# Local attention with 64 keys per 32 queries, a token shift in whole rows, and the band mask written into the score banks by ScalarE

## The reference

```python
for i in range(6):
    x = attn_layer(shift_tokens(x), Wqkv[i], ...) + x      # 16 heads of 64
    x = ffn_layer(shift_tokens(x), ...) + x                # 2 x 341 wide
# shift_tokens: the upper 64 of the 128 features come from the token before
# attention: q and k are normalised per head, rotated and scaled, then
mask = (it < jb) | (it > jb + w) | (jb == -1)              # w = 32
sim = jnp.where(mask, -jnp.finfo(sim.dtype).max, sim)
attn = softmax(sim); out = einsum(attn, v)
```

## Time and profile before

| | |
|---|---|
| median of 3 runs | 1836.76 us (1835.83 to 1837.04) |
| profiled execution, its own time | 1836.35 us |
| its span in the trace | 1834.6 us |
| PE, DVE, ACT, POOL busy | 1702.5, 1604.0, 1416.7, 1533.9 us |
| share of the span | 93%, 87%, 77%, 84% |
| mean granted TensorE clock | 0.979 of full speed |

### The profile page before, as it was taken

How to read it: one execution, slowest core, us unless ns; L and a number is a source line. 1 busy time by engine, 2 the same in 40 slices (tenths; PEclk the granted TensorE clock), 3 DMA queues, 4 the chain that set the end, 5 groups by cost and what they waited for, 6 DMA issues and landing times.

```text
span 1834.6 us, 39770 instructions
## 1 busy us (share of the span) xinstructions
PE 1702.5 (93%) x14065; PEld 1372.6 (75%) x14256; DVE 1604.0 (87%) x2852; ACT 1416.7 (77%) x4889; POOL 1533.9 (84%) x2056
## 2 busy tenths in 40 slices
PE   6589999999999999999999999999999999999995
PEld 4468777787787777787777877877777777778774
DVE  4588898998998989989989999989899899899982
ACT  3278878878788787787797787887877887978872
POOL 2489988898988988988989888889888889898870
PEclk9599999999999999999999999999999999999997
DMA  3000010000010000001000001000001000000000
GB/s 114 2 1 3 3 46 2 4 17 1 8 46 1 4 17 1 8 3 44 4 1 17 8 1 46 5 1 17 4 5 46 3 2 16 1 8 4 1 4 26
DMA packets 24154, 25.38 MB, mean 14 GB/s; under 512 B 13795, under 2 KB 21654, under 8 KB 23190
## 3 DMA queue, kind: packets, MB, share of 16 engines
q1 hardware_dynamic: 23958, 22.83, 4.1%
HBM read 18.65 MB, written 1.05 MB: 11 GB/s over the span
## 4 chain that ended last, share of the span: by engine, by line
PE 71%; DVE 19%; ACT 3%; issue 3%; POOL 3%; DMA 1%; SPq 0%; POOLq 0%; DVEq 0%
PE ps L410 9%; PE ps L382 8%; PE ps L402 7%; PE ps L369 7%; PE ps L390 7%; PE ps L362 7%; PE ps L364 5%; PE ps L363 5%; DVE xh L975 4%; PE ps L377 3%; PE ps L441 3%; DVE ss L905 2%; DVE t L920 2%; DVE t L922 2%; ACT pr L620 2%
## 5 line engine op out<-in xcount | busy, mean ns | idle before, releaser
L620 ACT ACTIVATE pr<-ps,nmax 128x128 f32<-128x128 f32 x1536 | 549.2, 389 | 28.2 <-DVE nmax L939 25.4
L743 POOL TENSOR_TENSOR t<-t 128x512 f32<-128x512 f32 x384 | 500.4, 1303 | 75.7 <-DVE t L922 75.7
L777 POOL TENSOR_TENSOR pr<-pr,rsum 128x512 f32<-128x512 f32 x384 | 406.5, 1059 | 22.8 <-DVE rsum L946 22.1
L765 POOL TENSOR_TENSOR t<-t,rn 128x512 f32<-128x512 f32 x384 | 402.5, 1048 | 21.8
L620 ACT ACTIVATION_READ_ACCUMULATOR pr<-ps,nmax 128x1 f32 x1536 | 352.4, 229 | 0.0
L585 ACT ACTIVATE sq<-ps 128x512 f32<-128x512 f32 x384 | 235.4, 613 | 116.0 <-PE ps L364 112.1
L920 DVE TENSOR_TENSOR t<-ps,rope 128x512 f32<-128x512 f32 x384 | 262.3, 683 | 42.0 <-ACT sq L585 37.5
L362 PE MATMUL ps<-w_hi,xt_hi 128*128 128x512 f32 x576 | 280.1, 486 | 14.3 <-DVE t L922 10.0
L369 PE MATMUL ps<-consts,t 128*128 128x128 f32 x1536 | 239.1, 278 | 29.4 <-ACT qT L612 26.1
L922 DVE TENSOR_TENSOR t<-ps,rope 128x512 f32<-128x512 f32 x384 | 260.5, 678 | 0.0
L905 DVE TENSOR_REDUCE ss<-sq 128x8 f32<-128x512 f32 x384 | 252.0, 677 | 3.6 <-ACT sq L585 2.6
(11 more groups left out here) (121 smaller groups left out, 2879.0 us busy)
## 6 DMA issues: line engine op xcount, KB each, us to landing
wqkv<-wqkv_in SPq DMA_DIRECT2D x6, 1536.0 KB, 12.3
wo<-wo_in SPq DMA_DIRECT2D x6, 512.0 KB, 9.6
xsh<-xr SPq DMA_DIRECT2D x24, 127.0 KB
w<-w_in SPq DMA_DIRECT2D x6, 342.0 KB, 7.5
w<-w_in SPq DMA_DIRECT2D x6, 172.5 KB
x<-x_in SPq DMA_DIRECT2D x4, 256.0 KB, 4.9
out<-x SPq DMA_DIRECT2D x4, 256.0 KB, 2.9
ctx<-ctx_in SPq DMA_DIRECT2D x4, 240.0 KB, 4.5
```

Of the source, the lines that this page charges most:

```text
L620: i = A(pr[:, g, k, :], ps[:, S_BANK[odd], k * P:(k + 1) * P], ACT.Exp, bias=nmax[:, h2, odd, k:k + 1], accum_out=psums[:, h2, odd, k:k + 1])
L743: G.tensor_tensor(t1[:, c, :], t1[:, c, :], t2[:, c, :], ALU.add).then_inc(qk_added[c], 1)
L765: G.tensor_tensor(w, w, rn[:, par(u), h2, a, :].unsqueeze(2).broadcast_to([P, 8, E]), ALU.mult).then_inc(done, 1)
L777: G.tensor_tensor(w, w, rsum[:, g // 2, g % 2, :].unsqueeze(2).broadcast_to([P, 4, P]), ALU.mult).then_inc(pr_ready[g], 1)
```

## The change

Scores and probabilities are made for only 64 keys for each 32 queries: the queries 0 to 31 and 32 to 63 take the keys from 0, 64 to 95 those from 32, and 96 to 127 those from 64. The parts are these.

- `scores` runs once in a unit, for all 16 heads: each head takes four matmuls of 32 queries by 64 keys. A group of 32 queries writes PSUM partitions of its own, so a head pair takes 8 places of the array. The mask is no longer a matmul. `mask_scores` (ACT) copies it into both banks, and the matmuls add to what stands there.
- `exps` has 16 activations of 64 columns, `row_max` runs once over both banks, `normalise_p` twice.
- Two heads' probabilities of 64 columns stand side by side, so `transpose_p` has 8 transposes in a unit in place of 16 and `copy_pT` two copies in place of four.
- `weigh_values` takes 48 matmuls over 64 keys, of 64 or 32 columns, in place of 16 over 128 keys. Transposed probabilities of even heads stand on partitions 0 to 63 and those of odd heads on 64 to 127, and so must the values: `shift_v` (SP) moves rows of v into `v_win` by four transfers of 64 rows by 512 numbers (128 KB) for each unit.
- `clamp_norm`, `guess_norm` and `refine_norm` run once in a unit for all 32 sums. `copy_o` runs twice on ACT and no longer on DVE.
- `shift_tokens` moves 127 whole rows of 512 numbers, where it moved 127 x 4 pieces of 64, and `copy_half` writes the lower half again after it, so it waits for the transfer.
- The weights of Q, K and V arrive in six transfers in place of one; w1 is split in two halves; the banks are dealt anew and all four `step` lists are written in another order.

```diff
+SPAN = 64
+WINDOW_START = [0, 0, 32, 64]
+BLOCKS = H // 2
...
-    QKV_BANK = [0, 1, 1, 0, 1, 0]
-    TQ_BANK = [4, 4, 5, 5]
-    TP_BANK = [4, 4, 5, 5]
-    O_BANK = [6, 6]
+    QKV_BANK = [1, 0, 1, 0, 0, 0]
+    TQ_BANK = [4, 5, 5, 4]
+    TP_BANK = [4, 5]
+    O_BANK = [6, 7]
...
-                sp.dma_start(xsh[1:P, :, E:P], xr[0:P - 1, s, E:P]).then_inc(f_shifted, 16)
+                sp.dma_start(xsh[1:P, :, :], xr[0:P - 1, s, :]).then_inc(f_shifted, 16)
+            def shift_v(u, odd):
+                sp.wait_ge(v_ready[odd], u + 1)
+                if u >= 2:
+                    sp.wait_ge(o_ps, 4 * (u - 1))
+                p, r = par(u), slice(E * odd, E * odd + E)
+                starts = WINDOW_START[1:3] if odd else WINDOW_START[2:4]
+                for n, t in enumerate(starts):
+                    sp.dma_start(v_win[r, p, n, :], v[t:t + SPAN, p, odd, :]).then_inc(v_shifted[odd][p], 16)
...
-            def scores(u, h2):
-                for odd in range(2):
-                    mm(ps[:, S_BANK[odd], :], ident16[:], band16[:].rearrange("p a k -> p (a k)"), start=True, stop=False,
-                       skip_group_check=True)
+            def scores(u):
+                for c in range(4):
+                    if c == Q1:
+                        pe.wait_ge(tq_ready[c], u + 1)
+                pe.wait_ge(band_ready, u + 1)
+                for c in range(BLOCKS):
+                    for g in range(P // WIN):
+                        for odd in range(2):
+                            r, q = slice(E * odd, E * odd + E), slice(WIN * g, WIN * g + WIN)
+                            i = mm(ps[q, S_BANK[odd], c * SPAN:(c + 1) * SPAN], qT[r, par(u), c, q],
+                                   kT[r, par(u), c, WINDOW_START[g]:WINDOW_START[g] + SPAN],
+                                   start=False, stop=c == BLOCKS - 1, skip_group_check=True)
+                            if c == BLOCKS - 1:
+                                i.then_inc(s_ps, 1)
...
+                even = [(0, 2 * WIN, v[0:E, p, 0]), (2 * WIN, WIN, v_win[0:E, p, 0]), (3 * WIN, WIN, v_win[0:E, p, 1])]
+                odds = [(0, 2 * WIN, v_win[E:P, p, 0]), (2 * WIN, WIN, v_win[E:P, p, 1]), (3 * WIN, WIN, v[E:P, p, 1])]
+                for j in range(BLOCKS // 2):
+                    for n in range(3):
+                        for b in range(2):
+                            for odd in range(2):
+                                c = 2 * j + b
+                                q, m, window = (even, odds)[odd][n]
+                                i = mm(ps[E * b:E * b + E, O_BANK[odd], j * P + q:j * P + q + m], window[:, c * E:(c + 1) * E],
+                                       pT[E * odd:E * odd + E, c, q:q + m], start=True, stop=True)
...
+            def mask_scores(u):
+                if u == 0:
+                    act.wait_ge(const_ready, 9)
+                else:
+                    act.wait_ge(exp_ready[3], u)
+                band = band16[:].rearrange("p c w -> p (c w)")
+                A(ps[:, S_BANK[0], :], band, ACT.Copy)
+                A(ps[:, S_BANK[1], :], band, ACT.Copy).then_inc(band_ready, 1)
...
             def copy_half(f):
-                pool.wait_ge(x_updated, f * QUAD + QUAD)
+                pool.wait_ge(f_shifted, 16 * (f + 1))
```

More of the change, by code:

```diff
@@ L104, in build @@
     kT = sb("kT", [P, 2, 8, P])
[L105 to L110, removed]
+    v = sb("v", [P, 2, 2, 512])
+    v_win = sb("v_win", [P, 2, 2, 512])
+    nmax = sb("nmax", [P, 2, BLOCKS])
+    psums = sb("psums", [P, H])
+    rsum = sb("rsum", [P, H])
+    pr = sb("pr", [P, BLOCKS, 2 * SPAN])
+    pT = sb("pT", [P, BLOCKS, P])
     oT = sb("oT", [P, 2, 8, P])
@@ L198, in run_input, with run_layer @@
             task((s - lag) // QUAD + NQ)
-    def at(s, lag, l):
-        return s - lag == l * B
+    def run_layer(s, lag, task, first=0, last=L):
+        if (s - lag) % B == 0 and first <= (s - lag) // B < last:
+            task((s - lag) // B)
     def par(u):
@@ L272, in _ @@
             sp.dma_start(vec[:], vec_d.rearrange("l p v -> p l v")).then_inc(ld_vec, 16)
[L273 to L286 removed]
+            for s in range(FIRST_STEP, LAST_STEP):
+                step(s)
             for q in range(NQ):
@@ L332, in cross_weigh @@
                 for b in range(QUAD):
-                    i = mm(ps[:, 7, b * P:(b + 1) * P], pT[0:CT, 0, b, :], xvv[:, q % 2, b, :], start=True, stop=True)
+                    i = mm(ps[:, 7, b * P:(b + 1) * P], pT[0:CT, b, :], xvv[:, q % 2, b, :], start=True, stop=True)
                 i.then_inc(c_o_ps, 1)
@@ L370, in transpose_qk @@
                 i.then_inc(tq_ps[c], 1)
-            def scores(u, h2):
-                if h2 == 0:
-                    pe.wait_ge(tq_ready[2 * h2 + 1], u + 1)
-                for odd in range(2):
-                    mm(ps[:, S_BANK[odd], :], ident16[:], band16[:].rearrange("p a k -> p (a k)"), start=True, stop=False,
-                       skip_group_check=True)
-                for k in range(4):
-                    for odd in range(2):
-                        r = slice(E * odd, E * odd + E)
-                        i = mm(ps[:, S_BANK[odd], k * P:(k + 1) * P], qT[r, par(u), 4 * h2 + k, :], kT[r, par(u), 4 * h2 + k, :],
-                               start=False, stop=k == 3, skip_group_check=True)
-                        if k == 3:
-                            i.then_inc(s_ps[h2], 1)
@@ new lines, in transpose_p, with weigh_values @@
+            def transpose_p(u, h2):
+                pe.wait_ge(pr_ready[h2], u + 1)
+                for k in range(4):
+                    i = tr(ps[:, TP_BANK[h2], k * P:(k + 1) * P], pr[:, 4 * h2 + k, :], ident)
+                i.then_inc(pt_ps[h2], 1)
+            def weigh_values(u):
+                p = par(u)
+                for h2 in range(2):
+                    if h2 == 0:
+                        pe.wait_ge(pt_ready[h2], u + 1)
+                    pe.wait_ge(v_shifted[h2][p], 32 * (u // 2 + 1))
+                even = [(0, 2 * WIN, v[0:E, p, 0]), (2 * WIN, WIN, v_win[0:E, p, 0]), (3 * WIN, WIN, v_win[0:E, p, 1])]
[8 more added lines that the diff above has]
+                                       pT[E * odd:E * odd + E, c, q:q + m], start=True, stop=True)
+                                if j == BLOCKS // 2 - 1 and n == 2:
+                                    i.then_inc(o_ps, 1)
@@ L644, in step @@
             def step(s):
+                run_quad(s, 9, ffn_gate, 2)
+                run(s, 3, copy_o, 0)
+                run(s, 2, exps, 0)
+                run(s, 2, exps, 1)
+                run_quad(s, 8, ffn_upper)
+                run(s, 0, square, Q0)
+                run(s, 0, upper_w, Q0)
+                run(s, 1, upper_w, V1)
                 run(s, 2, exps, 2)
```

507 lines of the change are left out of this document (236 added, 271 removed).

## The result

The changed kernel takes 1969.18 us (median of 4 runs, 1965.19 to 1980.57) where the kernel before takes 1836.61 (4 runs, 1835.83 to 1837.04). The ratio is 1.0732, interval 1.0688 to 1.0777: slower by 133 us, outside the range that the prediction gave. The profiled execution took 1968.4 us, its span is 1966.6.

The account below looks back on a forecast made before the run. PE and POOL were both taken as full in a 15.4 us plain step; afterwards waits between engines set 13.4, so 96 x 2.0 = 192 us off 1836 gives 1644 us, range 1530 to 1890.

Parts of the forecast that it names:

- The step that failed first: Token shift with fewer, longer rows, POOL's copy waiting for it: costs nothing, or up to 3 us a quad, 72 in all.
- The step that failed second: PE's small score and value matmuls: 3.3 us a unit, plus 0.4 for changes of layout.
- x: PE time of a unit's 64 score and 48 value matmuls, 224 records: taken as 3.3 us, bounds 2.3 to 15.2.
- weight loads take turns: PE's small matmuls: places in the same rows load weights in turn, 4.4 us, 1750 us; slow end of the 0.55 case.
- only two places work at once: Slower rival for PE's small matmuls: 6.3 us a unit, 1932 us; chance 0.21, shared with a fixed cost per record.
- The clock: Sign of error on PE: a lower clock because small matmuls fill the array less; no size given.
- The ring: Waits from mask through scores, values, result copies and exponentials back to mask, between ACT and PE: 13.4 us a step.
- A plain step: Step without feed-forward work: falls from 15.4 to 13.4 us.
- The mask copies: Two ACT copies a unit of the mask into the score banks: 0.48 us each, 0.96 for two.
- The transfers of v: Four 128 KB transfers a unit on SP: 3 us, hidden; a rival had them late, 1716 us, within a 0.03 chance.
- the 1644: Forecast time of the whole changed kernel in us: 1836 less 192.
- the third assumption that failed: Feed-forward work in three steps of a quad: costs the same as before, 9.4 us a quad over plain steps.

Follow-up runs that it names:

- experiment 1: Changed kernel with the token shift as two transfers of 112 and 15 whole rows in place of one of 127: 1847.92 us.
- experiment 4: Kernel before with only the token shift changed to one transfer of 127 whole rows, the POOL copy waiting for it: 2111.47 us, ratio 1.1505.
- experiment 11: As experiment 4, on the kernel before, but with the whole rows in two transfers of 112 and 15: 1845.23 us, ratio 1.0045.
- experiment 5: Separate kernel computing nothing of the reference: streams of small score-shaped matmuls, quiet, beside transfers, and between wide ones; 512 take 27.6 us quiet.
- experiment 8: On top of experiment 1, transposed probabilities and values rounded to bfloat16, so the block has 176 records in place of 224: 1741.85 us.
- experiment 10: On top of experiment 8, q and k rounded to bfloat16 too, so the block has 112 records: 1692.01 us, ratio 0.9212.
- experiment 3: On top of experiment 1, weighted values moved behind V1's projection late in the step, with a third buffer of v: 1878.56 us.
- experiment 7: On top of experiment 1, scores and weighted values split in halves between transposes and projections, with a third buffer for v: 1882.86 us.
- experiment 6: On top of experiment 1, the mask put in by two bfloat16 matmuls on PE again, without ACT mask copies: 1834.36 us, ratio 1.0000.
- experiment 9: The edits of experiment 6 and experiment 8 together: 1726.69 us, ratio 0.9399.

## Why the prediction was wrong

**The step that failed first** is the sentence on the token shift: "nothing, or up to 3 us a quad, 72 in all, if POOL were held". POOL was held, and the transfer takes 13 to 14 us, not 3. My 3 us came from transfers of 256 KB in the earlier trace rows, whose bytes are nearly the same; but bytes don't set its time (127 rows take 13.17 us, 128 rows 2.33), the number of rows and how it divides do. The earlier trace rows has no landing time for the token shift itself, and I filled the gap with a neighbour of another row count. The price is 121 us (experiment 1), 5.0 a quad. The same edit costs 276 us where POOL has no slack (experiment 4) and 9 when the rows are dealt out (experiment 11), so this cause is shown, in both kernels. Part of the price may come through the clock, which is at 0.925 in experiment 4 and at 0.982 in experiment 11.

**The step that failed second** is the cost of the small matmuls, in an unforeseen way. The bounds of x asked how fast the array takes them. There the forecast erred on the slow side; the timeline of PE in the changed kernel:

```profile
899.67 1.48 PE L409 MATMUL ps<-kT,qT 64*32 64x64 f32 x128
901.21 0.29 PE L438 MATMUL ps<-pT,v_win 64*64 64x64 f32 x4
902.63 0.26 PE L438 MATMUL ps<-pT,v_win 64*64 64x32 f32 x4 [1.13 <-issue]
...
904.03 0.49 PE L460 MATMUL ps<-xhT_hi,w_hi 128*114 128x512 f32 x1
```

The first values start at 901.09, so scores take 901.09 - 899.67 = 1.42 us for 128 records, 0.011 each. The values take 904.03 - 901.09 = 2.94, of which some 1.4 is the stop (902.63 - 901.21 = 1.42 from start to start, 1.13 of it idle). Four blocks of the changed kernel have no stop at all, and their first record is 2.94 to 3.01 us ahead of the next group: that is x with its changes of layout, where 3.3 + 0.4 was taken. Neither "weight loads take turns" nor "only two places work at once" happened: the latter would make scores 64 x 0.056 = 3.6 us. The prediction also cites 25 ns as the least from start to start from the Trainium skill ("TensorE: Matmul & The Clock Gate", Part 1, Wait - 56ns, not 53.3ns?); across eight places of the array the trace doesn't agree, starts lie 11 ns apart on average.

But the block of 224 records is 448 instructions in 3 us, and experiment 5 shows 256 supplied in 3.45 to 4.00. The forecast had no term for that. In experiment 1's trace, PE goes over 0.4 us without a start 97 times inside the block, about once a unit, 176 us in all; 4 of these are waits for the probability copies, and 91 lie an exact multiple of 256 instructions apart, PE's waits counted too. The scores and values of the kernel before have no such stop. Where in the block the multiples fall decides: 70 blocks cross two of them and all 70 stop at the second, 2 of these at the first too; 25 cross one, and 19 of them stop. With the block at 176 records 106 us go (experiment 8), at 112, where no block crosses two multiples, another 50 (experiment 10). Not all of this is supply: 48 value records fewer at 0.011 are 0.53 us a unit, 51 us at most, and 64 score records 68 at most. The stops fell by 66 us from experiment 1 to 8 (176 to 110), which with the 51 is 117, a little over the 106 measured. The bytes of v also halved there; the transfers are named in no wait of either run.

**The clock** was listed as a sign of error and shows. By an estimate from its two levels, (1 - 0.913) x 2 x 1966.6 = 342 us of the changed kernel ran at the lower one, (1 - 0.979) x 2 x 1834.6 = 77 before. The windows put these stretches behind stops of PE, not into the small matmuls, whose window 920 to 924 stands at 1.00; that small matmuls fill the array less, the reason given for the sign, no run shows as a cause. (In experiment 5, whose quiet stream stops for 1.4 to 2.3 us after every 256 instructions, small matmuls too ran at 0.50, from 32 to 52 us.) Experiment 11 is at 0.982 and experiment 1 at 0.935, but curing the stops at the instruction blocks doesn't bring the clock back: experiment 10, with 8 of them left, is at 0.919. There PE waits for DVE instead (for 1.26 us ahead of 899.47), and the clock is at 0.50 from 900 to 908. What these stretches cost by themselves was not isolated.

**What was right.** The ring is there: both attempts to move the values later lost time on ACT's result copies (experiments 3 and 7). A plain step is 12.36 without a stall, though 14.4 in the mean. A group of four exponentials starts 1.15 to 1.17 us before what follows it, against 1.22 forecast. The mask copies start 0.52 apart, and the next operation 0.52 behind, 1.04 for two, against 0.96:

```profile
897.79 0.61 ACT L658 ACTIVATE ps<-band 128x512 f32<-128x512 bf16 x1
898.31 0.60 ACT L659 ACTIVATE ps<-band 128x512 f32<-128x512 bf16 x1
```

The mask matmuls that replace them stand on the same ring, so taking the copies off ACT would give 96 x (0.96 - 0.43) = 51 us if the ring always bound; it gives 14 to 15 (experiments 6 and 9), so it binds in some steps only. The transfers of v land in 2.4 us and no view names a wait for v_win. POOL and DVE were relieved as forecast, and ACT's largest idle time is ahead of the result copies. One reading of the forecast is off without effect: 813.57 less 811.95 is 1.62, not 1.61.

**What the feed-forward part does.** Experiment 10 is free of most of both faults and still 48 us over the 1644. The plain step is not the reason (12.40 against 13.4). In the quad shown, four steps take 67.14, so three have 67.14 - 4 x 12.40 = 17.5 more than plain ones, not the 9.4 that I kept from the earlier trace rows. Averaged over its quads, from one residual of the same step to the next, it is 65.5 in all and a plain step 12.65, so 14.9 over: 5.5 x 24 = 132 more, against 0.75 x 96 = 72 less. That the feed-forward work costs the same on top of a shorter step was the third assumption that failed; why is not shown. One explanation is that a shorter step leaves less room in which that work can hide, with DVE at 42% of the chain. A rival is the clock: in the window of 67.14 us it is at 0.92, where the earlier trace rows has 1.00, and by an estimate from the two levels that is up to 0.08 x 67.14 = 5.4 us of PE's time, of the 17.5 - 9.4 = 8.1 that came on top. No run separates the two.

The rival on the other side, "only two places work at once" with 1932 us, came near in number and has nothing to do with what happened. Chances of 0.21 for slower rested on that mechanism; the two that decided were in neither list.

**A better version.** Experiment 9 beats both kernels, by 6.0% against before, with probabilities and values in bfloat16; experiment 10 by 7.9% with q and k so too. With all operands in float32 the best, experiment 6, equals the kernel before.

## What to carry to other kernels

Before an engine is made to wait for a transfer, look at the number of rows and not only at the bytes: 127 rows cost 13 us where 112 and 15 cost 2.5, and a transfer that was slow under cover before shows its whole length once something waits for it. When a change cuts matmuls into many small ones, count instructions as well as columns: here 256 were supplied in 3.45 to 4.00 us, and a block of 448 in 3 us stopped about once each time, however good the array's overlap, nearly always where it crossed a second multiple of 256; one of 224 hardly ever did. And when a gap is to be filled by reordering, check first whether the moved group is a link of the ring; two reorderings here shortened the gaps and lost more than they won.

## What was new about the hardware

- TensorE runs small matmuls in different places of the array at 0.011 us a record (128 in 1.42 us), all eight places of 64 rows by 32 columns included.
- Its instructions arrive in portions of 256, 3.45 to 4.00 us apart when they are needed faster; beside transfers of 128 KB the rate is about the same (512 matmuls in 26.7 us, and 27.6 without). Not every multiple of 256 has a stop: after 10.5 to 11.2 us of wide matmuls two of eight blocks of 448 instructions ran through in 2.42 us.
- SBUF to SBUF, 127 rows of 2 KB take 13.17 us, 128 rows 2.33, 113 rows 11.92, 112 rows 2.62.
- After a stop of 2.0 us in the block, and of 2.96 us ahead of the transposes behind the late transfer, the granted clock was 0.57 in the next 4 us although PE was busy for 4.00 and 3.59 of them.

Open are why a portion takes 3.45 us in one place and 4.00 in another, why some blocks of 448 instructions pass, what the stretches at the lower clock cost by themselves, and what sets the feed-forward steps of experiment 10.
